# A fused attention, expert and transformer kernel: feature maps in 32x64 tiles of TensorE, and the transformer pass in another order

## The reference

```
q, k, v = x @ Wq + bq, x @ Wk + bk, x @ Wv + bv        16 heads of 8 channels
x' = q * 8**-0.25 (and k alike);  u = x' @ omega (8 x 8 per layer, the same for all heads)
phi = [exp(u - |x'|^2/2), exp(-u - |x'|^2/2)] * 16**-0.5      16 features for each head
a = causal linear attention: (sum over j<=i of (phi_q_i . phi_k_j) v_j) / (sum of phi_q_i . phi_k_j + eps)
h1 = norm(x + a @ Wo + bo) * g1 + be1
out = norm(h1 + relu(h1 @ W1 + bf1) @ W2 + bf2) * g2 + be2
```

## Time and profile before

| | |
|---|---|
| median of 3 runs | 3515.63 us (3510.87 to 3519.11) |
| the profiled execution | 3509.98 us |
| its span | 3508.2 us |
| mean granted clock of PE | 0.973 |
| busy: PE, DVE, ACT, POOL | 3198.1, 2484.6, 1941.2, 1248.8 us |
| transformer, first turn to last turn of a slot | 1743.5 to 3069.3 us |

### The profile page before, as it was taken

One profiled execution on the slowest core, in us unless ns is written; L12 is line 12 of the kernel. 1 busy time (PEld: TensorE's weight loads), 2 busy tenths in 40 slices (PEclk: granted clock), 3 DMA queues, 4 the chain that ended last, 5 costly groups with the idle time before them and its releaser, 6 DMA issues. The chain is left out here.

```text
span 3508.2 us, 125238 instructions
## 1 busy us (share of the span) xinstructions
PE 3198.1 (91%) x53104; PEld 2420.4 (69%) x53104; DVE 2484.6 (71%) x6237; ACT 1941.2 (55%) x4014; POOL 1248.8 (36%) x980
## 2 busy tenths in 40 slices
PE   3999999999999998899889999999999999967998
PEld 2777777777777776677666767777776677745776
DVE  4776676677667776777667777777777777757775
ACT  2666666666666665666444555445555554525665
POOL 3333333333333332455513332323323323233554
PEclk9999999999999999999989999999999999988999
DMA  2000000000000000333200000000000000002333
GB/s 94 34 31 27 34 30 31 27 34 30 31 26 34 27 30 20 98 113 109 85 17 3 3 18 3 18 3 3 18 3 18 3 3 3 3 1 83 111 113 107
DMA packets 75861, 129.36 MB, mean 37 GB/s; under 512 B 11312, under 2 KB 21040, under 8 KB 74928
## 3 DMA queue, kind: packets, MB, share of 16 engines
q1 hardware_dynamic: 75312, 121.36, 10.6%
HBM read 85.15 MB, written 2.62 MB: 25 GB/s over the span
## 5 line engine op out<-in xcount | busy, mean ns | idle before, releaser
L673 ACT ACTIVATE a_prob<-a_s,a_shift,a_scale 128x128 f32<-128x128 f32 (+3 forms) x512 | 311.7, 613 | 239.7 <-DVE a_shift L759 228.6
L1783 POOL TENSOR_TENSOR ffn_weighed<-ffn_silu,ffn_shares 128x512 f32<-128x512 f32 x256 | 332.3, 1300 | 266.5 <-ACT ffn_silu L1747 245.7
L756 DVE TENSOR_REDUCE a_neg_max<-a_s 128x2 f32<-128x256 f32 (+3 forms) x256 | 209.2, 817 | 297.7 <-PE a_s L575 297.7
L977 POOL TENSOR_TENSOR t_rstd<-t_var_eps,minus_half 128x4 f32<-128x4 f32 x96 | 97.6, 1017 | 755.1 <-DVE t_var_eps L1352 755.1
L401 POOL TENSOR_TENSOR a_k_sin<-a_k_swap,sin_swap 128x512 f32<-128x512 f32 x64 | 82.8, 1294 | 776.9 <-DMA a_k_swap<-a_k_own 776.9
L1272 ACT COPY t_num<-t_n 128x512 f32<-128x512 f32 x96 | 56.2, 585 | 455.2 <-PE t_n L1059 454.6
L1899 DVE TENSOR_TENSOR ffn_ps_u<-ffn_weighed,ffn_ps_u 128x512 f32<-128x512 f32 x256 | 177.5, 693 | 155.6 <-POOL ffn_weighed L1783 154.2
L1420 DVE TENSOR_TENSOR t_mixed<-t_s,upto 128x512 f32<-128x512 f32 x384 | 238.2, 683 | 14.4 <-PE t_s L1035 12.7
L1747 ACT ACTIVATE ffn_silu<-ffn_ps_g 128x512 f32<-128x512 f32 x272 | 163.3, 600 | 128.8 <-PE ffn_ps_g L1637 112.7
L661 ACT COPY a_probT<-a_t 128x128 f32<-128x128 f32 (+3 forms) x512 | 194.0, 433 | 64.3 <-PE a_t L590 60.9
L1732 ACT CAST ffn_h_hi<-ffn_ps_u 128x512 fp32r<-128x512 f32 x272 | 159.3, 586 | 124.0 <-DVE ffn_ps_u L1899 117.8
(11 more groups left out here) (230 smaller groups left out, 8926.9 us busy)
## 6 DMA issues: line engine op xcount, KB each, us to landing
ffn_shares<-ffn_spread SPq DMA_DIRECT2D x256, 256.0 KB, 3.2
a_k_swap<-a_k_own SPq DMA_DIRECT2D x128, 128.0 KB, 2.1
a_y_swap<-a_y_own SPq DMA_DIRECT2D x128, 128.0 KB, 2.0
a_staged<-in_pairs SPq DMA_DIRECT2D x8, 384.0 KB, 3.1
t_next<-in_t_w SPq DMA_DIRECT2D x12, 256.0 KB, 3.0
t_next_rows<-in_t_rows SPq DMA_DIRECT2D x6, 448.0 KB, 4.1
x<-in_x SPq DMA_DIRECT2D x8, 256.0 KB, 5.0
out<-x SPq DMA_DIRECT2D x1, 2048.0 KB, 8.7
```

The costliest lines, as they stand in the source:

```text
L673: nc.scalar.activation(prob[c % 2][h][:, 0:(c + 1) * P], ps[f"s{h}"][:, 0:(c + 1) * P], ACT.Exp, bias=shift[:, k:k + 1], scale=scale[slot. ...
L756: nc.vector.tensor_reduce(neg_max[:, two], ps_s[:, :, 0:(c + 1) * P], AX.X, ALU.max, negate=True).then_inc(s["negs"], 1)
L1783: nc.gpsimd.tensor_tensor(weighed[n % 2][:], silu[n % 2][:], shares[k % RING][:], ALU.mult).then_inc(weighed_done, 1)
```

## The change

There are three parts.

The maps. ACT now evacuates q and k whole: one activation of 128 partitions for the plain values and one for the squares, `proj[j][0]` and `proj[j][1]`. `omega` becomes 128 rows by 64 columns and `half_norm` stands beside it as a table of its own. Each map is eight matmuls: for each strip of 32 rows one with omega (it opens the sum) and one with half_norm (it closes it), each with 32 rows, 64 output columns and 512 moving columns. Strips 0 and 1 write to the two halves of one bank's partitions, strips 2 and 3 to those of the other. The columns come out in the same places as before. The DVE copy that put half_norm into omega, and the semaphore for it, go; the staged omega is 128x64 and no longer 64x256.

The order on PE and POOL (SLOT): values goes behind Wo; mapk comes directly after mapq; A1 goes behind h1; nums goes ahead of F2. FIRST changes likewise. LEAD, TAIL and END stay.

The order on ACT and DVE: ACT takes A1 behind h1. DVE takes values behind Wo, between the statistics of the first norm and its normalising. On DVE nums stays behind F2.

```diff
@@ -782,13 +782,13 @@
 class TransformerPlan:
 
 
-    SLOT = ("turn att project values Wo mapq A1 mapk h1 keys weights F1 sums S0 F2 nums A0 S1").split()
+    SLOT = ("turn att project Wo values mapq mapk h1 A1 keys weights F1 sums S0 nums F2 A0 S1").split()
     LEAD = "turn project values mapq mapk keys sums S0 A0 S1".split()
-    FIRST = "turn project values mapq A1 mapk keys weights sums S0 nums A0 S1".split()
+    FIRST = "turn project values mapq mapk A1 keys weights sums S0 nums A0 S1".split()
     TAIL = "att Wo A1 h1 F1 F2 nums".split()
     END = "att Wo h1 F1 F2".split()
-    ACT = "turn att project mapq A1 mapk h1 kz weights F1 A0".split()
-    DVE = "values Wo Wo_norm keys weights F1 sums S0 F2 nums F2_norm S1".split()
+    ACT = "turn att project mapq mapk h1 A1 kz weights F1 A0".split()
+    DVE = "Wo values Wo_norm keys weights F1 sums S0 F2 nums F2_norm S1".split()
     WITH = dict(Wo_norm="Wo", F2_norm="F2", kz="mapk")
     FILLS = dict(weights="", turn="w0", project="w1 w0", values="n1", mapq="s0 s1", mapk="s2 s3", keys="w0 w1", sums="w0",
                  S0="s0 s1 s2 s3", S1="s0 s1 s2 s3", A0="n0", A1="n1",
@@ -829,7 +829,7 @@
 
         w_in = sb("w_in", [P, 3, P])
 
-        omega = sb("omega", [P, 2 * P])
+        omega = sb("omega", [P, SPAN])
         cols_in = sb("cols_in", [P, 2])
         bv = sb("bv", [P, P])
 
@@ -842,13 +842,13 @@
         be1_bf2 = sb("be1_bf2", [P, P])
 
         next_sq, next_1 = sb("next_sq", [P, 4 * P]), sb("next_1", [P, FT * P])
-        next_2, next_omega = sb("next_2", [P, FT * P]), sb("next_omega", [P // 2, 2 * P])
+        next_2, next_omega = sb("next_2", [P, FT * P]), sb("next_omega", [P, SPAN])
         next_cols, next_rows = sb("next_cols", [P, 4 + FT]), sb("next_rows", [P, 7 * P])
 
         o_now = sb("o_now", [P, TILES, P])
         oT = sb("oT", [P, SEQ])
 
-        proj = [[sb(f"{n}{t}", [P, SEQ]) for t in range(2)] for n in ("qq", "kk")]
+        proj = [(sb(n, [P, SEQ]), sb(n + "_squared", [P, SEQ])) for n in ("q", "k")]
         phi_q = [[sb(f"phi_q{t}_{i}", [P, SEQ]) for t in range(2)] for i in range(2)]
         phi_k = [sb(f"phi_k{t}", [P, SEQ]) for t in range(2)]
         kz = [sb(f"kz{t}", [P, SPANS, 2, SPAN]) for t in range(2)]
@@ -887,7 +887,7 @@
         w_loaded = sem("w_loaded")
         made_in = {n: sem("made_in_" + n) for n in ("act", "dve")}
         made_out = {n: sem("made_out_" + n) for n in ("act", "dve", "pool")}
-        ones_set, omega_set = sem("ones_set"), sem("omega_set")
+        ones_set = sem("ones_set")
         first = {"stats": sb("first_stats", [P, TILES, 6]), "mean_var": sb("first_mean_var", [P, TILES, 2]),
                  "var_eps": sb("first_var_eps", [P, TILES]), "rstd": sb("first_rstd", [P, TILES])}
         first_stats, first_mv, first_eps = sem("first_stats"), sem("first_mv"), sem("first_eps")
@@ -1096,10 +1096,16 @@
 
                         j = ("mapq", "mapk").index(step)
                         ready(("w1", "w0")[j], "project")
-                        for t_, bank in enumerate((("s0", "s1"), ("s2", "s3"))[j]):
+                        banks = (("s0", "s1"), ("s2", "s3"))[j]
+                        for bank in banks:
                             free(bank)
-                            nc.tensor.matmul(ps[bank][:], omega[:, chunk(t_)], proj[j][t_][:], start=True,
-                                             stop=True).then_inc(filled[bank], 1)
+                        for k, weights in enumerate((omega, mem["half_norm"])):
+                            for four in range(4):
+                                bank, at = banks[four // 2], SPAN * (four % 2)
+                                t = nc.tensor.matmul(ps[bank][at:at + SPAN, :], weights[strip(four), :], proj[j][k][strip(four), :],
+                                                     start=k == 0, stop=k == 1)
+                                if k and at:
+                                    t.then_inc(filled[bank], 1)
                     elif step == "keys":
 
                         for bank in ("w0", "w1"):
@@ -1204,9 +1210,6 @@
                     act.sem_inc(emptied[k], 1)
 
                 def weights_in(l, slot):
-                    if slot is None:
-                        act.wait_ge(omega_set, 1)
-                        act.nop(nofuse=True)
                     wait_staged(act, l, slot, "weights")
                     nc.scalar.copy(w_in[:].rearrange("p a n -> p (a n)"), next_sq[:, 0:3 * P])
                     nc.scalar.copy(cols_in[:], next_cols[:, 0:2])
@@ -1214,7 +1217,7 @@
                         def signed(ap):
                             return ap.rearrange("p (g s m) -> p g s m", s=2, m=8)[:, :, sign, :]
 
-                        t = nc.scalar.mul(signed(omega[0:64, :]), signed(next_omega[:]), (ROOT, -ROOT)[sign])
+                        t = nc.scalar.mul(signed(omega[:]), signed(next_omega[:]), (ROOT, -ROOT)[sign])
                     t.then_inc(made_in["act"], 1)
                     act.wait_ge(made_in["act"], l + 2)
                     act.nop(nofuse=True)
@@ -1244,12 +1247,8 @@
                     elif step == "project":
                         for j, bank in enumerate(("w1", "w0")):
                             full(bank)
-                            for t_ in range(2):
-                                half = slice(64 * t_, 64 * t_ + 64)
-                                nc.scalar.activation(proj[j][t_][0:64, :], ps[bank][half, :], ACT.Identity,
-                                                     bias=cols_in[half, j:j + 1])
-                                t = nc.scalar.activation(proj[j][t_][64:P, :], ps[bank][half, :], ACT.Square,
-                                                         bias=cols_in[half, j:j + 1])
+                            nc.scalar.activation(proj[j][0][:], ps[bank][:], ACT.Identity, bias=cols_in[:, j:j + 1])
+                            t = nc.scalar.activation(proj[j][1][:], ps[bank][:], ACT.Square, bias=cols_in[:, j:j + 1])
                             t.then_inc(emptied[bank], 1)
                     elif step in ("mapq", "mapk"):
                         j = ("mapq", "mapk").index(step)
@@ -1318,7 +1317,6 @@
                     t.then_inc(normed, 1)
 
                 first_part(0)
-                nc.vector.tensor_copy(omega[64:P, :], mem["half_norm"][64:P, :]).then_inc(omega_set, 1)
                 second_part(0)
                 first_part(1)
                 second_part(1)
@@ -2020,10 +2018,10 @@
     a["t_w1"] = t[f + "W1"]
     a["t_w2"] = t[f + "W2"].reshape(L, -1, P, P).transpose(0, 2, 1, 3).reshape(L, P, -1)
     heads, _, at = feature_places()
-    omega = np.zeros((L, P // 2, 2 * P), np.float32)
+    omega = np.zeros((L, P, P // 2), np.float32)
     for col in range(2 * P):
-        row = heads[col] % 8 * 8
-        omega[:, row:row + 8, col] = t[f + "omega"][:, :, at[col]]
+        row = heads[col] * 8
+        omega[:, row:row + 8, col % (P // 2)] = t[f + "omega"][:, :, at[col]]
     a["t_omega"] = omega
     columns = [t[f + n][:, :, None] for n in ("bq", "bk", "g1", "be1")]
     a["t_cols"] = np.concatenate(columns + [t[f + "bf1"].reshape(L, -1, P).transpose(0, 2, 1)], axis=2)
@@ -2054,7 +2052,7 @@
     key, query = i % (P // 2), j[:, :P // 2]
     heads, _, _ = feature_places()
     root = 8 ** -0.25
-    squares = (np.arange(P)[:, None] - P // 2) // 8 == heads[None, :] % 8
+    squares = np.arange(P)[:, None] // 8 % 4 == heads[None, :P // 2] % 4
     return {
         "upto": (key <= query).astype(f32),
         "half_norm": (squares * f32(-0.5 * root * root)).astype(f32),
```

## The result

The changed kernel takes 3551.98 us (median of four runs, 3550.05 to 3555.8). The kernel before took 3513.25 (3507.8 to 3519.11, four runs). The ratio is 1.0109, with a 95% interval of 1.0094 to 1.0124, which makes it 33 to 44 us slower. The forecast was 24 us on 3515.63. It had the sign, and the time lies inside 3500 to 3600. It also lies inside the forecast's own range (3528 to 3552), but by 0.02 us, which is luck. Its profiled execution took 3550.05 us, with a span of 3548.3 and a granted clock of 0.966.

What follows compares the result with a forecast made beforehand. PE set the pace before; a loop through PE, DVE and POOL would bind after. Regular slots and layer changes give +19 us for five layers, the first layer +6: sum +24, 3540 on 3515.63; range 3500 to 3600, own range 3528 to 3552.

Steps and rivals of the forecast that it cites:

- The loop: Each slot's round from h1 over F2, second norm, POOL's o_bias and first norm to next h1: 26.1 to 28.15 us.
- A1's 1.81: On PE, A1 moved between h1 and keys adds 1.81 us to the round from h1 to h1.
- Rival 1: PE stays the pace in all slots; each of 46 gains up to 0.87 us, giving 3476; chance 0.15.
- Rival 2: Map matmuls on PE run two at once, 3623 us, or one at a time, about 3950; chance 0.07.
- Rival 4: Errors in the slot count cancel, with a round near 27.6 us, giving 3516; chance 0.08.
- the first layer: DVE also norms incoming sequences there, so the longer path adds 3x1.95, +6 us; two slots around it gain about 1.
- rival 3: PE's clock falls after the new waits before h1: 3579 us if every second slot, 3618 if every slot; chance 0.20.
- The regular slots: Seven slots per layer outside the layer's change, each 28.15 against a mean of 27.55: 0.60 each, 4.2 us per layer.
- harms nothing by itself: Values queued on DVE behind the wait for o_bias cost nothing, since only A1 needs their bank, and comes late.
- Evacuations: ACT's eight activations of 64 partitions become four of 128: 2.8 us less per slot; PE saves 0.38 before mapq.
- the 0.49: On PE, A1 behind h1 gives ACT time for h1T, so F1's wait goes: 0.49 us saved per slot.
- Layer changes: In the slot of a layer's change PE's saving stands, less the later DVE path: an estimated -0.4 us each.

Runs made afterwards that it cites:

- Residual early: POOL makes the next slot's o_bias before scaling the finished sequence: against the changed kernel, 3505.18 us; the same edit against the kernel before, 3509.37 us.
- maps together: New maps in the order of the kernel before, except mapk straight behind mapq and A1 behind both, ahead of h1: 3490.26 us, ratio 0.9939 to the kernel before.
- filler: Changed kernel with two extra matmuls, their result unused, on PE ahead of h1's wait: 3563.79 us, ratio 1.0147 to the kernel before.
- order only: Kernel before with its old maps and evacuations, but the change's new order of steps: 3584.01 us, ratio 1.0210 to the kernel before.

## Why the prediction was right, and where its sizes were off

**The loop: right, in mechanism and size.** The forecast was 28.15 us for a turn (its printed terms add to 28.13), with PE's part 13.95; measured 28.11, with 13.97. The terms, one by one: nums 0.64 (0.64 by taking it out), handovers 0.09 and 0.06 for 0.06 and 0.1, from addition to normalising 3.41 for 3.48, since values fits wholly under POOL's power. Residual early in both kernels shows it as a cause: cutting the link on POOL gains 47 us where the loop was counted as binding, and nothing where it was counted as slack. A1's 1.81 is not shown alone: with A1 ahead of h1 PE's part fell by 1.51, since F1 took 0.30 back, and A1 stayed in the loop by its second way. Everything the prediction named as its sign is there: h1 waits 39 times for 43.4 us in all, L1446 begins 0.09 us behind the end of L973 with idle time ahead of it, regular intervals of 28.10 and more with none shorter, mapq and F1 without their waits, and the clock of the middle layers at 0.99.

**Rival 1, the loop does not bind:** fallen in this kernel. Its number for PE's own path was not far off, though. That path is 26.64 against 27.19 before, 0.55 less; I had counted 0.87 off a mean. It comes true in maps together, and residual early reaches the same 26.65 with the change's own order.

**Rival 2, the maps take turns:** fallen. A map takes 1.77 us where I took 1.9 and the one-after-another bounds were 3.6 and 7.3. It is even below the four-at-once bound of 1.82. The Trainium skill's rule ("TensorEngine Tiling (Array Packing)", "Restrictions and Gotchas") that different row tiles cannot access the same PSUM bank simultaneously, read as tiles that take turns, would have made it 3.6. The runs do not bear it out for tiles on disjoint partitions of a bank. They do not try tiles on the same partitions.

**Rival 4, the errors cancel:** fallen, with 3552 for its 3516.

**The term that was mis-sized: the first layer, +6 forecast, +12.4 measured, and the first h1 1.5 later.** Its four intervals are 31.55, 33.71, 33.96 and 30.91 against 29.54, 29.41, 29.46 and 29.29. The first of them grew by 2.0, near the 1.95 counted for the path. In the next three the clock, rival 3, came on top. PE's timeline there, in the changed kernel:

```profile
1848.13 1.11 PE L1187 MATMUL t_n<-ident,t_xn 128*128 128x128 f32 x4 [4.30 <-DVE t_xn L1357]
1849.18 0.44 PE L1059 MATMUL t_n<-t_mixed,t_v_pad 128*32 128x64 f32 x8
...
1852.54 0.81 PE L1118 MATMUL t_w<-ident,t_phi_k 64*128 64x64 f32 x16
...
1864.25 0.32 PE L1059 MATMUL t_n<-t_mixed,t_v_pad 128*32 128x64 f32 x8
```

PE had waited 4.30 us, and then h1 took 1849.18-1848.13 = 1.05 us where it takes 0.6, and A1 1852.54-1849.18 = 3.36 where it takes 1.8: both near twice. Both stand in the loop. From this h1 to the end of F2 are 1864.25-1848.13 = 16.12 us, where the regular slots take 13.97: 2.15 lost. The next two intervals take 16.34 and 16.33, behind waits of 5.14 and 5.16. Together that is 6.9 us. The windows view (length, busy time of PE, PEld, DVE, ACT and POOL, granted clock, DMA share, GB/s), changed kernel:

```profile
1848.50:1852.00 3.50, 3.50 (x112) 3.17 (x114) 0.00 (x0) 0.78 (x1) 2.26 (x2) 0.50 0.02 5
...
2089.52:2103.49 13.97, 13.60 (x324) 10.88 (x324) 9.09 (x19) 4.37 (x7) 2.56 (x2) 1.00 0.01 2
...
1831.00:1964.00 133.00, 114.59 (x2430) 85.80 (x2420) 95.65 (x292) 45.87 (x78) 37.33 (x32) 0.92 0.01 3
1961.00:3080.00 1119.00, 1037.40 (x22288) 758.72 (x22279) 820.39 (x2332) 442.90 (x773) 334.53 (x283) 0.99 0.03 7
```

and the kernel before:

```profile
1831.00:1961.00 130.00, 119.02 (x2350) 85.85 (x2345) 102.01 (x304) 65.81 (x106) 41.96 (x36) 0.99 0.01 3
```

Right behind the wait the granted clock is 0.50, the level of 1.2 GHz. The clock of the first layer fell as a mean from 0.99 to 0.92; that of the middle layers did not fall. Behind the wait of 1.70 us at 2089.52 it stayed at 1.00, behind the one of 4.30 it did not. The earlier trace rows showed a fall behind a wait of 1.91, and I carried that to all slots or to none; the first layer deserved its own term. The kernel before loses 1.7 us in the same way, in its fourth interval (13.51 from h1 to the end of F2 for 11.81). So the lower clock accounts for some 5.2 of the 12.4 us, and the other 7.2 stand near the path's forecast of +6. The filler points the same way: with it PE's stretches from h1 to the end of F2 lose 3.2 us in this layer in place of 6.9. A run that changes the clock alone was not made.

**The regular slots: 19.8 us from the loop, 27.0 in all.** For the 36 intervals the loop's 28.13 against the mean of 27.58 before gives 36x0.55 = 19.8; the forecast counted 35 slots at 0.60, 21. The other 7 are intervals above the loop's length. On PE, the stretches from h1 to the end of F2 hold 5.7 us above their shortest, 5.0 of it in four intervals with a stall, three in keys and one in A1. Two of them in the changed kernel's PE timeline, one in keys and one in A1:

```profile
2178.24 0.58 PE L1118 MATMUL t_w<-ident,t_phi_k 64*128 64x64 f32 x11 [1.02 <-issue]
...
2753.10 0.32 PE L1059 MATMUL t_n<-t_mixed,t_v_pad 128*32 128x64 f32 x8 [1.54 <-issue]
```

A1 was moved into the loop, and its stalls with it; keys stood in it before. The sum had no term for this: I compared a loop without stalls to a mean with stalls. Together with the first layer, and its first h1, this is nearly the whole distance between +24 and +39.

**Values "harms nothing by itself":** true in the forecast's order, where it even saves some 20 us. The prediction named its condition, that A1 comes late, and the condition counts: with A1 ahead of h1, values' late evacuation on DVE holds A1, and h1 behind it, for 0.74 us. My expectation for that run forgot it.

**Evacuations:** 149 us of ACT's busy time went, for 130 forecast; it took away mapq's 7.9 us of waits, which did not count while the loop bound. F1's 13.6 us went by A1's new place, and they counted: they are part of the 0.49 that the forecast took off the loop. **Layer changes:** -1.3 for -2, as forecast.

## What to carry to other kernels

Busy shares hide a loop through several engines whose length stands near that of an iteration. Add up its links, in this case from one h1 over F2, the norm, POOL and back, before moving a step of the critical engine into it. And keep unstalled lengths apart from means: idle time in front of a wait is where an engine's stalls vanish, and an edit that uses it up pays for them even when the loop has the same length. If a loop does bind, look for work on it that nobody waits for; here that was POOL's scaling of a finished sequence, and moving one addition ahead of it was worth 47 us.

## What the runs showed of the hardware that was not expected

Four 32-row strips ran at once however their matmuls were ordered: 1.77 us for a map with all omega products first, and 1.77 with both products of one bank first. Both maps took 3.64 us then, where strict order would have taken 4.55. So later matmuls passed earlier ones that were held up. The trace does not say whether the array did it or a step that put them in order before.

ACT's activations of 128 partitions follow each other faster than those of 64. Each takes the same 0.68 to 0.70 by its own record, but they start 0.58 us apart where the half ones started 0.69 apart. ACT's timeline in the changed kernel:

```profile
2081.63 0.69 ACT L1250 ACTIVATE t_q<-t_w,t_cols_in 128x512 f32<-128x512 f32 x1 [0.52 <-PE t_w L1087]
2082.21 0.68 ACT L1251 ACTIVATE t_q_squared<-t_w,t_cols_in 128x512 f32<-128x512 f32 x1
```

and in the kernel before, behind the first one at 2066.14:

```profile
2066.83 0.68 ACT L1251 ACTIVATE t_qq<-t_w,t_cols_in 64x512 f32<-64x512 f32 x1
```

Whether the partitions or the fact that the half activations wrote two halves of one tile makes the difference was not tried.

PE's stalls without a named releaser come in every kernel of the study, 16 to 23 us in the S steps alone between 1961 and 3080 us (17.0 before, 18.6 changed), and up to 2.0 us at once in A1 (order only). What causes them stays open.
